# Reading the second PSUM bank of a value unit before the sums are inverted, as two entries of the lists

## The reference, cut to what matters

```python
x = x + tanh(g_xattn[l]) * attention_l(layernorm(x), context)   # l = 0..3
x = x + tanh(g_ffn[l])   * feed_forward_l(layernorm(x))
# attention, l = 1, 2, 3
scores = einsum('bhqd,bhkd->bhqk', q, k) / sqrt(16)             # masked in 1 and 3
attn = softmax(scores)
ctx = einsum('bhqk,bhkd->bhqd', attn, v)                        # heads joined
return ctx @ Wo + bo
```

## Time and profile before

| what | value |
|---|---|
| median of 3 runs | 2409.64 us (2406.71 to 2410.01) |
| the profiled execution | 2409.89 us, its span 2407.8 us |
| TensorE clock granted | 0.998 of full on the mean |
| PE matmul busy | 2317.7 us, 24811 instructions |
| PE weight load busy | 1570.3 us |
| DVE busy | 1272.9 us |
| ACT busy | 1150.0 us |
| POOL busy | 844.9 us |

### The profile page before, as it was taken

One profiled execution on the slowest core, in us unless ns is written; L12 is line 12 of the kernel. 1 busy time (PEld: TensorE's weight loads), 2 busy tenths in 40 slices (PEclk: granted clock), 3 DMA queues, 4 the chain that ended last, 5 costly groups with the idle time before them and its releaser, 6 DMA issues. The chain is left out here.

```text
span 2407.8 us, 58090 instructions
## 1 busy us (share of the span) xinstructions
PE 2317.7 (96%) x24811; PEld 1570.3 (65%) x24811; DVE 1272.9 (53%) x2829; ACT 1150.0 (48%) x1758; POOL 844.9 (35%) x1522
## 2 busy tenths in 40 slices
PE   8999899999999998999999999899999999899999
PEld 4676455777777655676777655467777765557777
DVE  6545785554433577554542457664443346765432
ACT  5554476433345457443335546744233555765221
POOL 1332233443332233344432233334343223334342
PEclk9999999999999999999999999999999999999999
DMA  3200210000000000000000000000000000000000
GB/s 139 91 13 13 86 41 2 6 6 10 10 20 3 13 2 16 2 10 9 2 10 22 2 13 15 3 2 10 10 10 1 21 13 1 2 2 2 6 5 9
DMA packets 17470, 39.42 MB, mean 16 GB/s; under 512 B 1792, under 2 KB 11840, under 8 KB 16192
## 3 DMA queue, kind: packets, MB, share of 16 engines
q1 hardware_dynamic: 17216, 35.71, 4.3%
HBM read 29.78 MB, written 4.19 MB: 14 GB/s over the span
## 5 line engine op out<-in xcount | busy, mean ns | idle before, releaser
L1904 DVE TENSOR_REDUCE mx<-P 128x8 f32<-128x1232 f32 x256 | 367.3, 1435 | 208.0 <-PE P L1194 113.6
L1495 PE MATMUL P<-Et,w 128*128 128x256 f32 x1024 | 266.7, 383 | 0.2
L1495 PEld LDWEIGHTS P<-Et,w 128*128 128x128 f32 x1024 | 190.7, 190 | 65.5 <-issue 36.6
L1948 DVE SCALAR_TENSOR_TENSOR x<-P,w_first,x 128x512 f32<-128x512 f32 x96 | 71.9, 749 | 305.5 <-PE P L1354 120.1
L1607 ACT ACTIVATE Et<-x,sm 128x256 f32<-128x256 f32 x256 | 139.0, 592 | 143.2 <-POOL sm L905 142.3
L1653 ACT ACTIVATE ET<-P 128x2048 f32<-128x2048 f32 x96 | 180.1, 1876 | 51.4 <-PE P L1275 50.9
L1731 ACT ACTIVATE gu<-P 128x256 f32<-128x256 f32 x128 | 49.0, 383 | 271.2 <-PE P L1496 255.0
L1275 PE MATMUL P<-R,KB 32*128 32x256 f32 (+1 forms) x2560 | 153.8, 378 | 0.4 <-issue 0.3
L2113 DVE SCALAR_TENSOR_TENSOR gu<-gu,P 128x256 f32<-128x256 f32 x128 | 53.6, 419 | 189.9 <-ACT gu L1731 189.8
L1496 PE MATMUL P<-gu,b 128*128 128x256 f32 x512 | 152.3, 379 | 0.0
L1285 PE MATMUL P<-ET,VB 128*32 128x256 f32 x2048 | 143.0, 385 | 5.6 <-ACT ET L1653 3.0
(11 more groups left out here) (287 smaller groups left out, 4947.3 us busy)
## 6 DMA issues: line engine op xcount, KB each, us to landing
kvw<-in_wkv SPq DMA_DIRECT2D x12, 672.0 KB, 3.9
x<-in_x SPq DMA_DIRECT2D x16, 256.0 KB, 2.8
out<-x SPq DMA_DIRECT2D x16, 256.0 KB, 2.2
w<-in_w SPq DMA_DIRECT2D x2, 1024.0 KB, 6.9
w<-in_wexp SPq DMA_DIRECT2D x1, 1028.0 KB, 8.8
w_w<-in_wcon SPq DMA_DIRECT2D x1, 1024.0 KB, 11.1
w_w<-in_m3t SPq DMA_DIRECT2D x1, 1024.0 KB, 7.8
w<-in_w1q SPq DMA_DIRECT2D x1, 1024.0 KB, 9.8
```

What stands on the lines that cost most here:

```text
L1495: e.matmul(o, wm[:, c, js], s.xT[:, c, :], start=n == c == 0, stop=False, skip_group_check=True)
L1904: e.tensor_reduce(s.mx[:, i, :, 2 * u:2 * u + 2], quad[:, :, 0:2 * NK].rearrange("p g (a k) -> p g a k", a=2), AX.X, ALU.max).then_inc(q_d, 1)
```

## The change: nv in front of nz

The entry nz of DVE is cut in two. The new entry nv is the last read of bank k1 (the instruction of L1940), and it comes first. nz keeps the reciprocals and the transpose. turns() yields no, nv, nz, so that other entries of DVE can also stand between nv and nz. The estimates become 690 for nv and 985 for nz, where nz had 1655. The bank is given by nv, and PE waits for the first of the two counts of s.d_o instead of both. POOL still waits for both.

```diff
@@ parts, gives, place, late, turns
-    "nz": 1655
+    "nv": 690, "nz": 985
-    if (name, engine) in (("pv", "ACT"), ("nz", "DVE")) or READ.get(name) == engine ...
+    if (name, engine) in (("pv", "ACT"), ("nv", "DVE")) or READ.get(name) == engine ...
-    if name in ("pv", "no", "nz"):
+    if name in ("pv", "no", "nv", "nz"):
-    if name == "nz" and engine == "DVE":
+    if name == "nv" and engine == "DVE":
         return [("copied",)]
     yield "no", s, b, l
+    yield "nv", s, b, l
     yield "nz", s, b, l
@@ pe_program, pv
-    free[k1] = [(s.d_o, X.up(s.d_o, 2))]
+    free[k1] = [(s.d_o, X.up(s.d_o, 2) - 1)]
@@ dve_program
+def nv(s, b, l, k0, k1):
+    e.wait_ge(s.a_q, 10 * b + 2 * l + 4)
+    e.scalar_tensor_tensor(out=s.VS, in0=P[:, k1, :], scalar=tm[:, 3:4], in1=s.VS, op0=ALU.mult,
+                           op1=ALU.add).then_inc(s.d_o, 1)
 def nz(s, b, l, k0, k1):
     z = s.z.rearrange("p (b z) -> p b z", z=2)
     e.wait_ge(s.d_a, C.at(s.d_a))
     for n in range(2):
         e.reciprocal(z[:, :, n], s.Z[n]...).then_inc(d_own, 1)
     e.wait_ge(d_own, C.up(d_own, 2))
     e.transpose(s.Z[0], z.unsqueeze(3).broadcast_to([128, 16, 2, 16])).then_inc(s.d_o, 1)
-    e.wait_ge(s.a_q, 10 * b + 2 * l + 4)
-    e.scalar_tensor_tensor(out=s.VS, in0=P[:, k1, :], scalar=tm[:, 3:4], in1=s.VS, op0=ALU.mult,
-                           op1=ALU.add).then_inc(s.d_o, 1)
```

```diff
-"0230303232323232002022021012220221000331003310331330121212211232230202120320220132201313231323132300"
+"0323023023232332002022011022202221000331003103313330121212211223230202120320220132201313231332133001"
...
-"1333233333333333332332233221311211111211111111111111111221121222222222222222222222222222"
+"3133133333333333332332233221311211112111111111111111111221121222222222222222222222222222"
```

More of the change, by code:

```diff
@@ L276, in parts @@
             dve = {"grow": (160, 190, 230, 350, 620, 620, 620)[of[-1]] if name == "grow" else 0, "gb": 2400, "near": 350, "wide": 3180, "upt": 700, "tsum": 2250, "tern": 4500, "masks": 2750,
-                   "val": 460 if name == "val" and of[1] == 0 else 610, "norm": 885, "mx": 1357, "pv": 700, "no": 950 if l == 0 else 1240, "nz": 1655, "out": 700,
+                   "val": 460 if name == "val" and of[1] == 0 else 610, "norm": 885, "mx": 1357, "pv": 700, "no": 950 if l == 0 else 1240, "nv": 690, "nz": 985, "out": 700,
                    "down": 700, "gate1": 840, "top1": 1190, "lin": 800, "q1": 2090, "w1": 660, "am": 2170, "fin": 830,
@@ L340, in gives @@
                 return ["ET"]
-            if (name, engine) in (("pv", "ACT"), ("nz", "DVE")) or READ.get(name) == engine and (name != "no" or of[2]):
+            if (name, engine) in (("pv", "ACT"), ("nv", "DVE")) or READ.get(name) == engine and (name != "no" or of[2]):
                 return ["bank", "gated"] if name == "e3" else ["bank"] * (2 if name in ("st", "sts", "lin", "pv") or name == "qp" and of[2] == 0 else 1)
@@ L607, in build @@
[L607 to L616, removed]
@@ L632, in build @@
-            "DVE":
[L633 to L645, removed]
@@ new lines, in build @@
+                "3010303202203320010303201213222013212321301013033001313213212110320210100123032312303021010103101320"
+                "2003300120313230121320201313201330320330321020232020000010303100200202002000101100211321323032132332"
+                "3133133333333333332332233221311211112111111111111111111221121222222222222222222222222222",
+            "ACT":
+                "0000300132112322020020032033311121321230030102022022111231331330130202023213321301300302033223002101"
+                "1010310330011313100011012230323320333021110102213030202301320231200031131110300132021013123300320332"
+                "3011101212000100200201000202020031033213221320003103101011222111311111111200032300110312333333323330"
+                "2333313110112213033202222212222222223233330031222033130130012332232212000130321021220302330203011310"
+                "0102323132300033031102212121120133032302031211020012012302300103313330100130213023231121001013233010"
+                "3230020000020203030220020021011221312330001303032332023333331333332002011100330321111101111111113113"
+                "2333022230110321222222222222223121111010322120310103102321222132000130231202120023033203030111021032"
+                "1323000310313032122102101213330030203201120123120213020131033331301003130310212210101210023330323020"
+                "0003002020320002023020101212123133000330130302223133333333332100021100330132111111101111011213133332"
+                "2230111202232222222222212211110310321212103010303221222132000310231022120320330203011103010233123230"
+                "0033031102212120110123330032213012102003120213200131033331010301031230312120102011032303232030000220"
+                "303002020202030010211213231331333133333333133232221121111111111111112122222222222222222222",
@@ new lines, in build @@
+            "DVE":
+                "3232312302303230232020320202132310210300313222222311002221213312123032222323003322313100001031300221"
+                "0013030300301211211201010303321133331000330103310123202003032203101122102120103033121313212301013030"
+                "3132311030000131330102122323201211302112002020300220010000002010220333123320012112110113101311101110"
+                "1122120130220033313131030333332331333231131132112323222322322222222223322330330220220330220202112203"
+                "0033030110011003303223300101303123321120200311030113232201202010013123300322320101130021323132310303"
+                "1010112311330003031031130202220231203100200231200123320020030020002201131021213020332333303303330330"
+                "3331322213003210021101011331131131111111132321332133222122221222212122222121112110202022030320022211"
+                "2203003300310101100033322330101100312132332020013100311032300212001020213130322303223010113311323123"
+                "0130101013212331030010011303032122220332030022003322001200213000021002230011102321102303233303330330"
+                "3333303131222303210200111110011331111313111112321333132312212122222212222222211211211020202200323002"
+                "2211220300330301100110003322333001013103232311202003110301130320210001210221033322330220311130031132"
+                "3123013010101223113300013001130033212222023033202033212002001032010020022000301213012311233233133333"
+                "333333133122121112121111111111122112222222222222222222",
@@ L654, in build @@
+            "SP": "0300030013200000312000003120000312",
         }
@@ L758, in orders @@
                 back = list(bank.get(at_, ()))
-                if (p[2], p[1]) == ("DVE", "nz"):
+                if (p[2], p[1]) == ("DVE", "nv"):
                     back = back[1:]
@@ L2141, in dve_program @@
             stages = {"masks": masks, "gb": gb_, "grow": grow, "near": near, "wide": wide, "upt": upt, "tsum": tsum, "tern": tern,
-                      "val": val, "norm": norm, "mx": mx, "pv": pv, "no": no, "nz": nz, "out": out_, "down": down,
+                      "val": val, "norm": norm, "mx": mx, "pv": pv, "no": no, "nv": nv, "nz": nz, "out": out_, "down": down,
                       "gate1": gate1, "top1": top1, "lin": lin_, "q1": q1, "w1": w1_, "am": am, "fin": fin, "w2": w2_,
```

44 lines of the change are left out of this document (19 added, 25 removed).

## The result

The changed kernel takes 2412.68 us (median of 19 runs, 2408.14 to 2414.04), the kernel before 2409.39 us beside it (19 runs, 2405.89 to 2411.21). The ratio is 1.0014, with a 95% interval of 1.0008 to 1.0020. The runs of before fall into two groups, 7 at 2405.9 to 2406.8 us and 12 at 2408.2 to 2411.2, while all but one of after's take 2410.7 us or more. The change cost 3.3 us where the forecast had a gain of 6.9.

The account below looks back on a forecast made before the run. PE bounds the kernel, losing 151.6 us in four dense stretches (220 us per batch, attentions of layers 1 to 3) where DVE's pieces come late. 2409.89 - 6.2 - 1.8 + 1.1 = 2403.0 us; own range 2399.5 to 2406.5, whole 2394 to 2416.

Parts of the forecast that it names:

- The DMAs of SP change by one swap of neighbours and are not in the neck.: SP's DMA queue: two neighbouring entries swap places, away from the bottleneck; no term in the sum.
- What the search changed in stretches without these units I count as nothing: New lists outside units with the split piece: counted as 0, as the trace cannot tell an order from its neighbour.
- 145: Sign: PE's idle time plus fills in the four 220 us dense stretches falls from 151.6 to about 145 us.
- Bank k1 earlier: PE's bank k1 comes free 1.03 us sooner in 35 dense-stretch units, 36.1 us of bank time: gain 6.2 us.
- The rule of 17% of the bank time: Bank time priced at the dense stretches' share without useful PE work, 17%: 6.2 of 36.1 us.
- Room between nv and nz: On DVE, maxima right behind the product in ten units could start 1.03 us sooner: gain 1.8 of 10.3 us.
- DVE's stand at nv: DVE waits for ACT's copy before the product, 6.5 us more than the 4.5 before: cost 1.1 us.
- Slower, by the clock: Rival: new lists open half-clock holes in the other three dense stretches, 3 x 3.6 us: 2413.8 us, chance 0.08.
- Slower, by the stand at nv: Rival: PE feels all 6.5 us of DVE's added wait for ACT's copy, earlier bank unneeded: 2416.4 us, chance 0.13.
- Nothing: Rival: bank release stays hidden and the lists' promised gain goes in small delays: 2409.9 us, chance 0.22.
- PE gets no later work from POOL's product: POOL's inputs come at most 0.2 us later, covered by PE's other work: counted 0, far bound 7 us.

Follow-up runs that it names:

- best kernel: The changed kernel with SP's mask copies put back in front of the kvw load and three of POOL's bias additions moved: 2402.39 us, ratio 0.9973 to before.
- late release: Best kernel with nz right behind nv in DVE's list, and PE waiting for both counts of s.d_o before it uses bank k1: 2409.98 us.
- old piece: Best kernel with reciprocals, transpose and product run as one piece at nv's place, and PE waiting for both counts of s.d_o: 2407.51 us.

## Why the prediction was wrong

The forecast was 2403.0 us. The kernel that has the split and the new lists without the two side effects takes 2402.4; the changed kernel takes 2412.7. With the side effects as each measured alone, 2409.5 - 7.1 + 6.1 + 4.5 = 2413.0.

The step that failed is the one on what else the search moved. The sum has three terms, all of the split, and puts every other swap at nothing:

- *"The DMAs of SP change by one swap of neighbours and are not in the neck."* There are two swaps, and one puts some 16 us of DMA issues behind a load that waits for its buffer. It cost 6.1 us. All that was needed was in the strings and in the trace of before: the place of `late` in SP's list, the start of kvw's load for layer 3 (335.6 us), and the start of the first scores that use these masks (350.5 us).
- *"What the search changed in stretches without these units I count as nothing"*, with the reason that the trace can't tell an order from its neighbour there. For the stretches with such units the sum has no term for other swaps either, and gives no reason. All three new holes (350, 1518 and 2104 us) lie in the dense stretches. POOL's order around 1514 and 2100 us cost 4.5 us. In the trace of before one can see DVE's instruction of L2033 take 0.62 us for two numbers a row, ending 0.03 us behind an addition of POOL (1514.64 + 1.26 = 1515.90), and the next tensor_scalar take 0.21 with POOL idle. I didn't look at durations that differ without a reason.

That 2403.0 lies so near to the best kernel's 2402.4, and 145 to its 145.2, is partly luck. Some 2 us of that kernel's gain are not the split's (not told from nothing), and the terms of the split gave a fair total from sizes that were off:

- **Bank k1 earlier:** -6.2 forecast, -2.4 measured (uncertain). The rule of 17% of the bank time was too generous; PE's added wait with the late release is 4.0 us.
- **Room between nv and nz:** -1.8 forecast, -5.1 measured. I priced only the maxima right behind (ten); just four came between, and PE's waits for maxima fell by only 0.5 us. So the mechanism of this term was wrong too. Moving nz away also changed what else of DVE was on time.
- **DVE's stand at nv:** +1.1 forecast, +2.5 by the difference of the kernels with the old piece and with the product first (2407.51 and 2409.98, both with the late release; intervals overlap). The stand rose by 10.3 us there and by 15.4 in after. In the old lists the same order, with the earlier bank, cost nothing.
- **Together** -5.0 where -6.9 was forecast. This is no second measurement: the three differences lead from the best kernel to the one with the old piece, and add up to its 5.1 us by construction. What two kernels show directly is that the first and the third cancel.

The rivals. *Slower, by the clock* gave 2413.8 and came nearest, by luck. Three new stretches at half clock did appear, but one of them in the first dense stretch and not one in each of the others. Its 10.8 us for three holes met the 10.6 us that the waits and the clock cost together, of which the clock is 4.3, and the holes weren't the planner's: they followed waits for SP's copies and for DVE's slowed chain. *Slower, by the stand at nv* is refuted as the cause of the loss: the best kernel has the whole stand of 19.8 us, and in the old lists a stand of 10.8 us moved nothing. *Nothing* is refuted for the split as a whole by the 5.1 us to the old piece in the same lists, but its picture of a hidden release fits the old lists, where the product first with the earlier bank changed nothing. The range, 2394 to 2416, held the time; the forecast's own, 2399.5 to 2406.5, did not.

That PE gets no later work from POOL's product was right: 1.2 us in 3 waits, before and after. The reason was not whole: I had the inputs of POOL at most 0.2 us later, but its wait for them rose from 172.9 to 205.4 us in 40 units, most of it where other entries stand between nv and nz (171.6 in 39 with nz right behind nv). The cover held all the same.

## What to carry to other kernels

When a change brings newly searched lists, price the lists too: go through the queues with few entries, DMA queues first, entry by entry, and ask of each one that moved what it now stands behind and who needs it, above all where the planner knows of no dependence. A single entry put back, or moved in the old kernel, shows the cost of one swap in one run. Judge a structural change with such side effects taken out, or a gain of 7 us is filed as a loss of 3 (of the 7 here, 5 are the split's).

## What the runs showed of the hardware

- DVE's tensor_scalar instructions with operands in on-chip memory are held up by POOL's tensor_tensor of 1.27 us, and by a memset of 0.31 us right behind it: 0.21 us became 1.36, and a chain of 2.1 us alone became 5.9 beside four additions in a row. A reduction beside an addition kept its 0.69 us. Over the best kernel the additions add 7.6 us to DVE's busy time, and about 2.6 us to the end.
- SP issues copies within on-chip memory 0.63 us apart, so 24 small ones take 15.4 us of queue time (16.0 in after), and are a long entry in a queue that looks empty.
- The clock makes a wait dearer. PE's stands of 4.4 and 4.7 us were each followed by a few us at 1.2 GHz, and matmuls without a use, put where PE stood, kept the clock and took 4.3 us off.
